# First feed-forward layer as two float32r products, and V stored with nine columns a head

## What is computed

```python
def _conn_dense(kernel_bool, x):
    w = jnp.where(kernel_bool, 1.0, -1.0)
    return x @ w
def _L0_ffn_ref(x, k0, k1, k2, s0, s1, s2):        # 128 -> 512 -> 512 -> 128
    h = jnp.concatenate([x, -x], axis=-1)
    h = s0 * _conn_dense(k0, h);  h = relu(h) * 2
    h = s1 * _conn_dense(k1, h);  h = relu(h) * 2
    return s2 * _conn_dense(k2, h)
x = x + attn_a(layernorm(x));  x = x + ffn(layernorm(x))
x = x + attn_b(layernorm(x));  x = x + ffn(layernorm(x))
```

## Time and profile before

| what | us |
|---|---|
| median of 3 runs (lowest, highest) | 3251.58 (3245.51, 3251.91) |
| the profiled execution, its own time | 3252.7 |
| its span, first to last instruction | 3251.0 |
| PE busy / ACT busy / DVE busy / POOL busy | 2633.0 / 2331.9 / 2122.2 / 617.5 |
| mean granted TensorE clock | 0.908 of 2.4 GHz |

### The profile page before, as it was taken

One profiled execution on the slowest core, in us unless ns is written; L12 is line 12 of the kernel. 1 busy time (PEld: TensorE's weight loads), 2 busy tenths in 40 slices (PEclk: granted clock), 3 DMA queues, 4 the chain that ended last, 5 costly groups with the idle time before them and its releaser, 6 DMA issues.

```text
span 3251.0 us, 72995 instructions
## 1 busy us (share of the span) xinstructions
PE 2633.0 (81%) x22579; PEld 1202.3 (37%) x22579; DVE 2122.2 (65%) x10282; ACT 2331.9 (72%) x3225; POOL 617.5 (19%) x797
## 2 busy tenths in 40 slices
PE   1778788888879887888888888798878888887666
PEld 1211243334433444334433344333433344333454
DVE  1730468856689467866678566894678766893595
ACT  1579567986689676996679766896769967796433
POOL 2000012401132011311124011320113111321231
PEclk8579688999999998999989999899989999999888
DMA  1101000100001000000001000010000000000000
GB/s 47 38 8 56 11 2 8 47 21 8 3 33 33 13 9 9 32 29 14 5 9 47 22 8 2 32 33 13 9 9 31 29 13 6 9 2 1 1 8 8
DMA packets 60333, 58.23 MB, mean 18 GB/s; under 512 B 14962, under 2 KB 41268, under 8 KB 59940
## 3 DMA queue, kind: packets, MB, share of 16 engines
q1 hardware_dynamic: 59940, 53.34, 5.3%
HBM read 35.66 MB, written 17.56 MB: 16 GB/s over the span
## 4 chain that ended last, share of the span: by engine, by line
PE 40%; ACT 23%; issue 20%; DVE 11%; POOL 4%; SPq 1%; ACTq 0%; DMA 0%; DVEq 0%; POOLq 0%
PE banks L749 37%; ACT PT L1074 11%; DVE pq L1223 3%; ACT pq L1061 3%; POOL Aop L728 2%; PE banks L769 1%; DVE xn L1408 1%; ACT xn L1032 1%; ACT h L1086 1%; DVE h L1411 1%; ACT h L1133 1%; POOL qkf L702 1%; ACT hparts L1085 1%; PE banks L974 1%; ACT Bs L1001 1%
## 5 line engine op out<-in xcount | busy, mean ns | idle before, releaser
L1074 ACT ACTIVATE PT<-banks 128x1024 f32<-128x1024 f32 x1024 | 996.6, 1035 | 51.8 <-PE banks L749 43.0
L1223 DVE CUSTOM_DVE_ANT_0 pq<-pq,banks 128x512 f32<-128x512 f32 x1024 | 660.4, 685 | 295.9 <-ACT pq L1061 269.3
L1061 ACT ACTIVATE pq<-banks 128x1024 f32<-128x1024 f32 x512 | 523.5, 1022 | 346.0 <-PE banks L749 333.9
L749 PE MATMUL banks<-K,Q 48*128 48x512 bf16 x3072 | 494.8, 435 | 111.3 <-ACT pq L1061 64.9
L749 PE MATMUL banks<-PT,Vg 128*32 128x512 f32 x4096 | 561.9, 621 | 2.0 <-ACT PT L1074 2.0
L749 PE MATMUL banks<-Q,K 51*128 51x512 bf16 x2048 | 398.8, 397 | 166.5 <-ACT PT L1074 156.7
L712 POOL TENSOR_TENSOR hparts<-h,hparts 128x512 fp32r<-128x512 f32 x112 | 140.3, 1271 | 1151.6 <-ACT h L1086 1151.4
L1408 DVE MATCH_REPLACE8 xn<-h,xn 128x96 f32<-128x96 f32 x1536 | 353.1, 248 | 0.0
L749 PEld LDWEIGHTS banks<-Q,K 51*128 51x128 bf16 x2048 | 109.4, 93 | 591.9 <-issue 562.1
L749 PE MATMUL banks<-hparts,W 128*128 128x512 f32 x1024 | 301.9, 423 | 27.2 <-ACT h L1086 20.3
L749 PEld LDWEIGHTS banks<-K,Q 48*128 48x128 bf16 x3072 | 127.0, 100 | 422.4 <-issue 365.3
(11 more groups left out here) (200 smaller groups left out, 3408.7 us busy)
## 6 DMA issues: line engine op xcount, KB each, us to landing
scratch_qk<-pq SPq DMA_DIRECT2D x8, 1536.0 KB, 6.1
qkf<-in_hidden_states SPq DMA_DIRECT2D x16, 512.0 KB, 3.8
Q<-scratch_qk SPq DMA_DIRECT2D x128, 48.0 KB
K<-scratch_qk SPq DMA_DIRECT2D x128, 48.0 KB
Q<-scratch_qk SPq DMA_DIRECT2D x128, 32.0 KB
K<-scratch_qk SPq DMA_DIRECT2D x128, 32.0 KB
out<-xr SPq DMA_DIRECT2D x14, 256.0 KB, 2.3
Q<-scratch_qk SPq DMA_DIRECT2D x128, 16.0 KB
```

What stands on the lines that cost most here:

```text
L749: return pe.matmul(o, l, r, start=start, stop=stop)
L1061: act.activation(cut(g), ring_pair if work is TURN0 and g % 2 else pair[0], ACT.Relu).then_inc(diff_out.sem, 1)
L1074: act.activation(PT[:, at:at + 2, :], pair[g % ESLOTS], ACT.Exp, scale=1.0 if i % 8 < 4 else -1.0).then_inc(probs.sem, 1)
L1223: dve.tensor_tensor_reduce(r, r, pair[1 + g % 2][:, par, :], 1.0, -3.0e38, ALU.subtract, ALU.max, mred[:, par, i, qt:qt + 1]).then_inc(max ...
```

## The change

`W0` becomes float32r. Where a half is turned (`lnT`, but for the norms that feed the windowed attention), ACT first evicts the bank into `hi` in float32r, then into `xT` in float32 as before. POOL subtracts: `lo` = `xT` - `hi`, in float32r. Each `fa` is then two accumulating float32r matmuls, `W0` times `hi` and `W0` times `lo`; the weights 0, 2 and -2 are exact in that type. In the first of the four `fa`, PE waits between the two matmuls for `lo` (two new counters, for p and for q and z). `Vg` has nine columns a head in place of 32, the output of head j covers nine partitions from 32j, and the memset to zero on POOL goes. `qparts` and `bparts` are names for memory that Q and B also use.

```diff
-        W0 = sb("W0", [P, NF])
+        W0 = sb("W0", [P, NF], F32R)
+        with nc.sbuf_tensor("qparts", [P, 2, 2, 2, HALF], F32R) as qparts:
+            pass
-        Vg = sb("Vg", [P, NU, NH, VW])
+        Vg = sb("Vg", [P, NU, NH, HD + 1])
+        with nc.sbuf_tensor("bparts", [P, 2, 2, HALF], F32R) as bparts:
+            pass
         B = sb("B", [P, 2, RPAD])
+        def in_parts(work, side, half):
+            parts = qparts[:, 1] if work is LAST and side in ("q", "z") else bparts
+            return parts[:, half, 0], parts[:, half, 1]
+        xlow_p = count("low_rows_p", 2)
+        xlow_q = count("low_rows_q", 2)
-            link(pool.memset(Vg[:, :, :, :], 0.0))
             link(pool.memset(Vg[:, :, :, HD:HD + 1], 1.0))
...
+                    if stage == "lnT" and n[0] != 1:          # GpSimd
+                        hi, lo = in_parts(work, side, n[1])
+                        pool.wait_ge(*R.moved(c, k))
+                        pool.tensor_tensor(lo, xT_[:, HALF * n[1]:HALF * n[1] + HALF], hi.bitcast(F32),
+                                           ALU.subtract).then_inc((xlow_p if side == "p" else xlow_q).sem, 1)
...
-                            ins = mm(ov_bank[i // 8][VW * j:VW * j + VW, :], ...
+                            ins = mm(ov_bank[i // 8][VW * j:VW * j + HD + 1, :], ...
...
-                        one(c, k, [(R.bank(k)[:, :], W0[:, P * o:P * o + P], xT_[:, HALF * (n % 2):HALF * (n % 2) + HALF], True, True)])
+                        hi, lo = in_parts(work, side, n % 2)
+                        pe.wait_ge(*R.free(c, k))
+                        mm(R.bank(k)[:, :], W0[:, P * o:P * o + P], hi, True, False)
+                        if o == 0:
+                            pe.wait_ge(*(xlow_p.at(b, n + 1) if side == "p" else xlow_q.at(b, n % 2 + 1)))
+                        mm(R.bank(k)[:, :], W0[:, P * o:P * o + P], lo, False, True).then_inc(R.ready.sem, 1)
...
-                        evict(c, k, xT_[:, HALF * n[1]:HALF * n[1] + HALF], R.bank(k)[:, :])
+                        act.wait_ge(*R.filled(c, k))
+                        if n[0] != 1:
+                            act.activation(in_parts(work, side, n[1])[0], R.bank(k)[:, :], ACT.Identity)
+                        act.activation(xT_[:, HALF * n[1]:HALF * n[1] + HALF], R.bank(k)[:, :],
+                                       ACT.Identity).then_inc(R.emptied(k), 1)
```

More of the change, by code:

```diff
@@ L870, in go @@
                         for j in range(4):
-                            ins = mm(ov_bank[i // 8][VW * j:VW * j + VW, :], Vg[:, i % 8, 4 * n + 2 * (j // 2) + j % 2, :],
+                            ins = mm(ov_bank[i // 8][VW * j:VW * j + HD + 1, :], Vg[:, i % 8, 4 * n + 2 * (j // 2) + j % 2, :],
                                      PT[:, (4 * s + j) % (2 * PT_SLOTS), :], i % 8 == 0, i % 8 == 7)
```

## The result

The changed kernel takes 3268.99 us (median of 13 runs, 3261.2 to 3277.1), the kernel before, run beside it, 3251.58 (13 runs, 3242.62 to 3257.3). The ratio is 1.0052, with a 95% interval of 1.0040 to 1.0064: some 17 us slower. 3250 was forecast, with 3265 as the upper end of the range, so the forecast missed, and on the side that had 0.22. The profiled execution took 3264.4 us (span 3262.5), 11.7 more than the one of before; its mean granted clock is 0.881 against 0.908.

What follows compares the result with a forecast made beforehand. PE was taken as the bound between places where a half is turned, ACT inside them. Place terms 6.0-3.6-0.6-0.6-0.5-2.0 = -1.3 us, with some 1.5 us gained from V, led to 3250 us; the 8-in-10 range was 3236 to 3265.

Steps and rivals of the forecast that it cites:

- the side that had 0.22: Whole kernel: chance given to a slower result, above 3258.1 us; made of most of C and D, with E.
- In all PE loses 128 x 0.41 = 52 us of work: First-layer matmuls (fa): each takes 0.41 us less PE time, 52 us in all, little of it on the path.
- q's half 0: Phase one, q's first half, six places: -0.95 in three turns, -0.4 in two, 0 in one; -3.6 us.
- p's half 0: Phase one, first layer norm of p's first half, once a turn: +1.0 each, all on the path, +6.0 us.
- ACT's second eviction: Where halves are turned: starts 0.58 us after the first; +0.6 at q half 1, 0.15 reaching PE at p half 1.
- Rival D: Added ACT work exposed at p half 1, q half 0, turn 1 and tail: +11 us, 3261; 6%.
- p's half 1: Phase one, p's second half, six places: low part hidden, 0.15-0.25 us each, -0.6 in all.
- Rival C: Clock falls at the new low-part wait at six p half 0 places: +12 us, 3262; 20%.
- Rival A: TensorE's time is the path: all or part of 52 us goes; credible form -17, 3235; 16%.
- V: Products with V in phase two: nine-column weights load faster, some 1.5 us gained from ACT's waits for PE.
- Rival B: Phase two: V's narrow loads count in full, -12.8 us, 3239; 11%.

Runs made afterwards that it cites:

- Experiment 9: Changed kernel without low part, its wait and ACT's second eviction; each first-layer product is hi twice: 3246.61 us, ratio 0.9992 to the kernel before.
- Experiment 10: Experiment 9 with two useless matmuls on hi ahead of each first-layer product: 3236.38 us, ratio 0.9969 to the kernel before.
- 11: Changed kernel with two useless float32r matmuls on hi ahead of each first-layer product: 3257.08 us, ratio 1.0030 to the kernel before.
- 5: Changed kernel with four useless matmuls on hi ahead of the first fa of a half 0 and of the last group: 3270.57 us, ratio 1.0076.
- 12: Changed kernel with VectorE making the low part from PSUM, one ACT eviction, and two useless matmuls ahead of each product: 3261.0 us, ratio 1.0041.
- experiment 1: Kernel before with only V's edits (nine columns a head), first layer still in float32: 3243.43 us, ratio 0.9985.
- experiment 3: Changed kernel without POOL's subtraction and PE's wait; both ACT evictions stay, each product is hi twice: 3257.16 us, ratio 1.0036.
- experiment 4: Changed kernel with first-layer matmuls in float32 from xT again; hi eviction, subtraction and wait kept but their parts unused: 3287.17 us, ratio 1.0123.
- experiment 6: Changed kernel with two parts at half 1 only; half 0 in float32 from xT with one eviction: 3252.87 us, ratio 1.0015.

## Why the prediction was wrong

Two steps failed: the clock was held constant while work was taken off PE, and ACT's second eviction was priced too low.

- **The clock: "In all PE loses 128 x 0.41 = 52 us of work. The rows show how little of it is on the path."** That little of it is on the path was right. It was then carried as worth nothing to the end, while the granted clock of the earlier trace rows was taken to stay. Experiment 9 shows that this work held the clock up: without it 769 us instead of 592 lie at 0.50, and every later matmul in those stretches is longer. Put back, it is worth 7 to 12 us (experiments 10 and 11), though two other fillers gained nothing (5 and 12). The cue stood in the earlier trace rows, a stretch of phase one at 0.50 and another of the same turn at 1.00; I used it to price matmuls and not to ask how near the others are to falling.
- **q's half 0, forecast at -3.6, is of the other sign.** I had three turns at half clock, two between and one at full clock. Before, the first result came at 3.40 us in four of the six and at 2.76 in turn 4, where 1.81 is full clock (experiment 1), so none was that. For turn 4 I had 0: ACT starts 3.32 us after the eviction instead of 2.76, for 3.02 worked out, and as the window at 1481 shows the stretch is now at 0.50; the scores behind it are 7.22-5.90 = 1.3 us later. In the four turns the first result does come earlier, by 0.08 us where 0.15 was worked out. But the second layer is later in all six, 8.5 us in all, with the clock at 0.50 for 10 to 11 us behind the first fa.
- **p's half 0, forecast at +1.0,** came to 8.16-6.84 = +1.3. The first 3.03 us are the forecast's to 0.01; the 0.3 more arise behind them, in the stretch that is at half clock from 1559.2 on. But the sum of six places did not arrive at the end of the turns: phase one grew by 0.4 us or so in turns 3 to 6. The sum added up places as if nothing closed behind them, and in these turns something does.
- **ACT's second eviction**, the other failed step, was spread over the places as 0.15 or 0.6 us and set off against a faster fa, with -1.3 as the sum. With the short matmuls it costs 10 to 14 us (experiment 3 against 9), the largest single term; with the long ones 4. Rival D, which priced it at +11 and had 6%, was nearest in size here, but not at the places that it named (at p's half 1 the second layer starts 0.2 to 0.4 us sooner after the eviction than before); that ACT is idle 74 of 198 us did not protect it, as it is idle at other times.
- **Rival C** (20%, 3262) named the right mechanism, and its sign stands in all six turns: p's half 0 goes to 0.50 behind the wait, 37.5 us in all where experiment 9, without the wait, has none. But it took the wait for the only cause. Experiment 3 takes the wait away and keeps the low clock; from there to the changed kernel only 742.6 to 777.1 us are added, since the halves 1 get back more than half of what the halves 0 lose. And with fp32 matmuls the same wait leaves more of the clock (experiment 4, 667.3). The Trainium skill, "TensorE: Matmul & The Clock Gate", in the section "A second HAM failure mode: psum-queue depth-cycling", has short idle times between groups of matmuls as enough to make the clock swing between its levels. I had weighed one gap only. p's half 1 of experiment 9 agrees with this section: three short gaps of 0.17 to 0.42 us between shorter groups, and then a wait of 1.47 us behind which the clock is at 0.50, where 1.42 us behind longer groups without gaps leave it at 1.00.
- **Rival A** (16%) fell: no part of the 52 us is to be seen, even alone (experiment 9 against 1). Experiment 10 is 0.0016 or 5 us below experiment 1 with intervals that overlap, but it is no case for A: with its fillers a fa takes PE 4 x 0.26 = 1.04 us against 0.93, and ACT's first result at p's half 0 comes at 1.88 us against 1.81. If the gain is real, its reason stays open.
- **V was forecast at -1.5** and is -5 (experiment 1, 2 to 8 by its interval); phase two is 5.1 us shorter in the profiled executions. The load's 20 ns are within the 25 that I allowed. What was too small is the worth of a wait: I took 15 ns off each of ACT's 12 waits a phase two, and they fell from 5.3 to 3.6 us, 140 ns each. Rival B's -12.8 was too much.
- **Right were** the bodies of the instructions: 0.26 from fa to fa at full clock, POOL's 1.27 us, 3.03 us to the first result.

## What to carry over

Work taken off TensorE between waits that other engines set may save nothing there, and can lower the granted clock for all that follows: before taking it off, look at how the clock stands in the windows around it, and where the mean is already below 1, count the unedited matmuls at half clock as the other end of the range. A quick test of that is a version that does the removed work uselessly; if it is faster, the clock is part of what the change costs; if only the clock rises, as in experiments 5 and 12, it settles nothing. The place of a fall is as telling as the mean: read the clock at the same place in every turn and every version. An eviction added to an engine that is idle a third of the time is not priced by the idle share; look whether it stands between two engines at that place.

## What the runs showed of the hardware that was not expected

- Useless matmuls made two kernels faster: 3246.61 to 3236.38 us (clock 0.882 to 0.912), and 3268.99 to 3257.08 (0.881 to 0.909). They made none faster in two others, though the clock rose there too (experiments 5 and 12).
- Two fa of float32r at half clock take 2.06 us, two of fp32 at full clock 1.97 (experiments 9 and 1, at the same place): fewer passes that bring the clock down buy nothing there.
- The mean clock alone does not order the kernels: experiment 4 has 0.899 and is the slowest, experiment 9 has 0.882 and is level with the kernel before (0.9992 [0.9975, 1.0010]). A direct delay can outweigh the clock, as in experiment 4.
- Shorter fa bring the half clock to their own places: with short fa at half 1 only (experiment 6), the halves 1 have 57.9 us at 0.50 in turns 2 to 7, against 6.6 in experiment 1, and the halves 0 have 12.8 against 22.0.
